# Causal linear attention in 64-token chunks instead of 128-token tiles, on one core of a Trainium2

## The reference

```python
q, k, v = (phi(qkv[0]), phi(qkv[1]), qkv[2])      # phi(x) = elu(x) + 1
def step(carry, inp):
    S, z = carry
    q_t, k_t, v_t = inp
    S = S + k_t[..., :, None] * v_t[..., None, :]
    z = z + k_t
    num = einsum('bhde,bhd->bhe', S, q_t)
    den = maximum(sum(z * q_t, axis=-1, keepdims=True), EPS)
    return (S, z), num / den
out = einsum('bld,ed->ble', out, w_out)
x = x + ga * out                                   # then the experts on layernorm(x)
```

## Time and profile before

| | |
|---|---|
| median of 3 runs | 864.46 us (862.91 to 868.9) |
| profiled execution, span | 864.3 us |
| PE busy | 812.9 us, 94% of the span |
| DVE, ACT, POOL busy | 577.1, 488.9, 478.9 us |
| instructions | 24637 |

### The profile page before, as it was taken

One profiled execution on the slowest core, in us unless ns is written; L12 is line 12 of the kernel. 1 busy time (PEld: TensorE's weight loads), 2 busy tenths in 40 slices (PEclk: granted clock), 3 DMA queues, 4 the chain that ended last, 5 costly groups with the idle time before them and its releaser, 6 DMA issues.

```text
span 864.3 us, 24637 instructions
## 1 busy us (share of the span) xinstructions
PE 812.9 (94%) x9527; PEld 667.7 (77%) x9527; DVE 577.1 (67%) x1740; ACT 488.9 (57%) x1003; POOL 478.9 (55%) x621
## 2 busy tenths in 40 slices
PE   6899999999999999999999999868999998999994
PEld 4677776777767767777777677558999998999994
DVE  5676676777777867868767767750756655767762
ACT  4665666656757656657657565442655453555551
POOL 2203345664664665646656646564556657666654
PEclk9999999999999999999999999988999999999997
DMA  5589903333332233322222212334476666676653
GB/s 195 186 247 282 284 26 114 85 87 110 67 120 89 76 114 87 86 101 70 72 71 62 64 50 41 62 85 148 82 158 120 151 145 122 152 152 158 121 100 37
DMA packets 71426, 99.02 MB, mean 115 GB/s; under 512 B 7810, under 2 KB 52866, under 8 KB 71320
## 3 DMA queue, kind: packets, MB, share of 16 engines
q1 hardware_dynamic: 38744, 53.93, 23.0%
q0 software_dynamic: 21760, 31.66, 16.2%
q10 hardware_dynamic: 10816, 11.96, 4.5%
HBM read 46.84 MB, written 63.36 MB: 127 GB/s over the span
## 4 chain that ended last, share of the span: by engine, by line
PE 75%; POOL 6%; DMA 6%; DVE 4%; issue 4%; ACT 3%; POOLq 0%; another core or an unknown queue 0%; SPq 0%; DVEq 0%; ACTq 0%
PE PJ L1436 10%; PE SCW L1662 9%; PE MD L1409 7%; PE SCW L1340 7%; PE SCW L1376 7%; PE PJ L1446 5%; PE SCW L1677 4%; PE SCW L1360 4%; PE SCW L1401 4%; DMA out<-EX,desti 3%; PE MD L1350 3%; PE SCW L1366 2%; PE SB L1677 2%; PE MD L1677 2%; POOL hT L544 2%
## 5 line engine op out<-in xcount | busy, mean ns | idle before, releaser
L494 POOL DMA_INDIRECT slot_rows<-Hrow,sloti x128 | 128.0, 1000 | 129.6 <-PE SCW L1366 48.5
L967 DVE TENSOR_TENSOR Sm<-SCW,tri 128x1024 f32<-128x1024 f32 x128 | 150.7, 1219 | 70.9 <-PE SCW L1340 69.0
L612 POOL DMA_INDIRECT out<-EX,desti x80 | 125.3, 1566 | 24.1 <-POOL idle L440 11.4
L1436 PE MATMUL PJ<-hT,w_qkv 128*128 128x512 f32 x384 | 110.1, 419 | 2.4 <-POOL hT L544 1.9
L440 POOL TENSOR_TENSOR idle<-mhalf 128x1 f32<-128x1 f32 x136 | 58.9, 433 | 78.5 <-DVE EX L1270 47.2
L1436 PEld LDWEIGHTS PJ<-hT,w_qkv 128*128 128x128 f32 x384 | 69.7, 190 | 25.1 <-issue 6.5
L1376 PE MATMUL SCW<-Sm,VA 128*17 128x128 f32 x2048 | 80.8, 275 | 0.2 <-issue 0.2
L1409 PE MATMUL MD<-w_og,ATs 128*128 128x256 f32 x256 | 73.2, 404 | 4.7 <-ACT ATs L824 2.8
L676 ACT ACTIVATE EX<-PJ 128x512 f32<-128x512 f32 x64 | 37.9, 592 | 67.5 <-PE PJ L1436 67.5
L1340 PE MATMUL SCW<-QM,KT 32*128 32x256 f32 x1024 | 73.3, 400 | 0.6 <-ACT OTs L839 0.5
L680 ACT ACTIVATE N<-X,nb,rs 128x256 f32<-128x256 f32 x128 | 66.4, 591 | 12.3 <-POOL nb L554 12.2
(11 more groups left out here) (215 smaller groups left out, 1825.4 us busy)
## 6 DMA issues: line engine op xcount, KB each, us to landing
Hrow<-slot_rows SPq DMA_DIRECT2D x32, 516.0 KB
slot_rows<-erow ACTq DMA_DIRECT2D x1, 10400.0 KB, 46.7
X<-x SPq DMA_DIRECT2D x16, 512.0 KB, 4.8
out<-X SPq DMA_DIRECT2D x16, 512.0 KB
Hrow<-mod_rows SPq DMA_DIRECT2D x16, 512.0 KB
QT<-slot_rows SPq DMA_DIRECT2D x8, 516.0 KB
slot_rows<-Hrow,sloti POOLq DMA_INDIRECT x128
N<-wd SPq DMA_DIRECT2D x4, 512.0 KB
```

Of the source, the lines that this page charges most:

```text
L494: pool.indirect_dma_start(xe, bass.IndirectOffsetOnAxis(sloti[:, par, k, t:t + 1], 0), Hrow[:, par, t, :], None, bounds_check=last_slot, o ...
L612: pool.indirect_dma_start(out, bass.IndirectOffsetOnAxis(desti[s % 2][:, a:a + 1], 0), Ys[s % 2][:, a, :], None, bounds_check=TOK - 1, oob ...
L967: dve.tensor_tensor(o.rearrange("p c (k w) -> p c k w", k=2), SCW[:, 2 * pair:2 * pair + 2, :].rearrange("p k (c w) -> p c k w", c=DC), tr ...
L1436: last = mm(PJ[m % 2][:], w_qkv[:, wp, cc, m * P:(m + 1) * P], hT[:, hp, cc, :], start=(cc + i == 0), stop=(cc == DC - 1 and i == len(SPLI ...
```

## The change

The chunk in which the attention is exact within itself shrinks from 128 to 64 tokens; a slot still holds one tile, which is two chunks (k = 0, 1).

- `scores` makes, for each chunk, 64 keys by 64 queries for two parities of heads: 16 matmuls of 32 rows x 64 columns of the array that stream 128 columns, instead of 8 of 32 x 128 that stream 256. The masked scores are 1024 numbers per partition instead of 2048, and DVE masks them with one instruction.
- `from_state` has 16 matmuls that stream 64 columns instead of 8 that stream 128: each chunk has its own state.
- `from_tile` has 32 matmuls of 64 rows x 17 columns (placed as 64 x 32) that stream 64 columns, instead of 16 of 128 rows that stream 128, and is no longer split.
- `add_to_state` has 16 matmuls of 64 rows instead of 8 of 128, into PSUM banks that it overwrites, and runs one tile ahead (tile n+1 in slot n). DVE masks both chunks' sums (`Snew`), then adds them one after the other to the state in SBUF (`Sbd`, now four states), three instructions instead of one. The product with the identity is gone.
- The keys of tile n+1 and the columns of tile n-1 are transposed together (`columns_and_keys`, four transposes), and ACT copies both with one instruction of 512 numbers instead of two of 256.
- `head_rows` moves to the end of the attention part of the same tile's slot, and DVE normalises the heads in that slot.
- PSUM: MD and PJ1 are now the two halves of PM, and each also takes the sums of one chunk; the output product goes to SB. So `add_to_state` waits until PJ1 has been read, and the late part of stage 1, the transposes of stage 1, the logits and `head_rows` wait for the new semaphore `state_read`. Several of POOL's sends of rows wait for other semaphores than before, and the second layer norm's scales are made one slot earlier.

```diff
+CH = P // 2
-        tri = sb("tri", [P, 2, P])
+        tri = sb("tri", [P, P])
+        tri64 = sb("tri64", [P, CH])
-        PJ = [ps("PJ0"), ps("PJ1")]
+        PJ0 = ps("PJ0")
+        PM = ctx.enter_context(nc.psum_tensor("PM", [P, 2, 512], F32))
+        PJ, MD = [PJ0[:], PM[:, 0, :]], PM[:, 1, :]
...
+            def columns_and_keys(n):
+                c0, c1 = (0 if tile_ok(n - 1) else D), (2 * D if tile_ok(n + 1) else D)
+                act.wait_ge(ak_full, n + 2)
+                at_least(act, op_full, n - 1)
+                at_least(act, state_full, n + 1 if tile_ok(n) else n)
+                act.activation(AK[:, c0:c1], MD[:, c0:c1], ACT.Copy).then_inc(ak_done, 1)
...
+            def masked_scores(T):
+                dve.wait_ge(sc_full, T + 1)
+                at_least(dve, av_done, T - 1)
+                dve.tensor_tensor(Smh(T % 2), SCW[:, :, 0:2 * P].rearrange("p r (m i) -> p r m i", i=CH),
+                                  tri64[:].unsqueeze(1).unsqueeze(1).to_broadcast([P, 4, 4, CH]),
+                                  ALU.mult).then_inc(sm_done, 1)
...
+            def state(n, first, second):
+                t = n + 1
+                dve.wait_ge(state_full, t + 1)
...
+                dve.tensor_tensor(Snew[:], PM[:, :, 0:DC * 2 * SW].rearrange("p k (h w) -> p k h w", h=DC * 2),
+                                  headmask[:].unsqueeze(1).to_broadcast([P, 2, DC * 2, SW]), ALU.mult
+                                  ).then_inc(state_read, 1)
...
+                dve.tensor_tensor(state_at(2 * t + 1), state_at(2 * t), Snew[:, 0], ALU.add).then_inc(sbd_half, 1)
...
+                    dve.tensor_tensor(state_at(2 * t + 2), state_at(2 * t + 1), Snew[:, 1], ALU.add).then_inc(sbd_done, 1)
...
+            def scores(T):
+                pe.wait_ge(q_masked, 2 * T + 2)
+                at_least(pe, ot_done, T)
...
                 for cc in range(DC):
+                    for k in range(2):
+                        for r in range(4):
...
+                            last = mm(SCW[part(k), r, cc * P:(cc + 1) * P],
+                                      KT[rows, gp, cc, q * P + CH * k:q * P + CH * k + CH],
+                                      QM[rows, T % 2, :, cc, part(k)], start=True, stop=True, skip_group_check=True)
...
+            def columns_and_keys(n):
...
+                    pe.wait_ge(an_done, n)
...
+                        last = pe.transpose(MD[:, cc * P:(cc + 1) * P], a[:, cc * P:(cc + 1) * P], ident[:])
...
+                    at_least(pe, ak_done, n + 1)
...
+                        last = pe.transpose(MD[:, D + cc * P:D + (cc + 1) * P],
+                                            KT[:, (t // 4) % 2, cc, (t % 4) * P:(t % 4 + 1) * P], ident[:])
...
+            def from_tile(T):
...
+                for cc in range(DC):
+                    for b in range(2):
+                        for k in range(2):
+                            for a in range(4):
+                                r, s = 2 * b + a // 2, a % 2
+                                last = mm(OB[32 * a:32 * a + SW, k, b, cc, :], VA[part(k), gp, q, head(cc, r, s), :],
+                                          Smh(T % 2)[part(k), r, 2 * cc + s, :], start=False, stop=True,
+                                          skip_group_check=True)
...
+            def add_to_state(n, g, routed, step):
...
+                pe.wait_ge(ak_done, n + 2)
...
+                        if n % 4 == 1:
+                            pe.wait_ge(h_raw, 2 * N + 2)
+                        else:
+                            pe.wait_ge(pj_read, 6 * N + 2 * (n % 4) - 2)
...
+                    if routed and step == "columns":
+                        pe.wait_ge(h2t_done, 2 * g + 2)
+                    if routed and step in ("first", "pick"):
+                        pe.wait_ge(taken, g + 1)
...
+                for cc in range(DC):
+                    for k in range(2):
+                        for r in range(4):
...
+                            last = mm(PM[32 * r:32 * r + 32, k, cc * 2 * SW:(cc + 1) * 2 * SW],
+                                      Kn[part(k), cc * P + 32 * r:cc * P + 32 * r + 32],
+                                      VA[part(k), gp, q, h:h + 2, :].rearrange("p s w -> p (s w)"),
+                                      start=True, stop=True, skip_group_check=True)
...
             def head_rows(T):
-                pe.wait_ge(ot_done, T)
-                at_least(pe, x1_done, T - 1)
+                pe.wait_ge(ot_done, T + 1)
+                pe.wait_ge(state_read, min(T + 2, TILES))
```

485 lines of the change are left out of this document (227 added, 258 removed).

## The result

The changed kernel takes 928.14 us, the median of 4 runs (924.81 to 929.81), against 865.19 us for the kernel before (4 runs, 862.91 to 868.9) on the same chip: a ratio of 1.073, 95% interval 1.069 to 1.077. The forecast was 831 us, the range 797 to 862, and 0.09 stood on slower. Nearly all of the 63 us lies in the attention stage: from the first to the last start of the scores pass 592.0 us (30.0 to 622.0), and 531.0 before (25.7 to 556.7). (Some executions of a kernel take over 1.5% longer than its fastest; medians here count them, ratios leave them out.)

What follows compares the result with a forecast made beforehand. The prediction took PE's list of steps to bound the kernel: -4.9 + 0.8 + 1.35 + 0.7 = -2.05 us per group, over 16 groups -33 us, from 864.3 to 831 us; range 797 to 862.

Steps and rivals of the forecast that it cites:

- What bounds the kernel: Attention stage: PE's own list of steps sets the time, busy 33.61 of 34.86 us of one group.
- PE's steps: PE's attention steps fall from 3.66 to 2.48 us a tile, identity product gone: 4.9 us saved per group.
- the form: PE step time is streaming rounds on side-by-side array places plus a rest; from the tile and sums 0.78 us.
- Instruction supply: From the tile and sums: small matmuls outrun the pace at which instructions arrive, +0.8 us per group.
- Instruction fetches: PE's 16 KB instruction packets: 1.7 times as many, partly visible in the small-matmul block, +1.35 us per group.
- Handovers: Waits between engines in the new order, chiefly add_to_state and stage 1's transposes: +0.7 us per group, bounds 0 to 2.
- A: Rival: PE's instructions keep up, no supply loss, fetches hidden as today; -4.25 us per group, 796 us, chance 0.20.
- B: Rival: only four array places work side by side, scores and from the tile stream as before; 851 us, chance 0.10.
- C: Rival: ACT becomes late for the slot, a quarter of a microsecond in every slot; 847 us, chance 0.12.
- D: Rival: small-matmul block runs at the arriving pace and every fetch shows; +1.7 us per group, 892 us, chance 0.13.
- L1389 plus L1422: Sign: product from the tile plus the sums on PE take near 1.0 us between starts.
- "issue" waits of PE: Sign: PE's waits for nothing the profile shows become about four times as many, in block L1374 to L1422.

Runs made afterwards that it cites:

- e13: Changed kernel with tile sums before the product from the tile in every slot, only the first two gate fills, output writes after the last tile: 886.0 us, ratio 1.033.
- e5: Changed kernel with the tile sums moved ahead of the product from the tile in every slot, not only q = 0: 906.7 us, ratio 1.049.
- e3: Changed kernel with only the first two gate fills and all output writes held back until the attention stage's last tile: 903.0 us, ratio 1.048.
- e7: Kernel before with its four attention products cut into as many matmuls as the changed kernel, without SyncE's bulk transfers in the attention stage: 923.3 us, ratio 1.069.
- e16: e15 with only the first two gate fills and output writes after the last tile: 902.2 us, ratio 1.057.
- e15: Changed kernel, sums first, half the fills, tile-wise writes, ScalarE reordered; output product behind sums, head rows between halves of late stage 1: 916.7 us, ratio 1.074.
- e9: Changed kernel with 32 more transposes on PE before the first tile, shifting the later code: 937.5 us, ratio 1.088.
- e6: Kernel before, order, tile and transfers kept, with its four attention products cut into as many matmuls as the changed kernel: 938.2 us, ratio 1.085.

## Why the prediction was wrong

**What bounds the kernel**: right. PE's list set the time before, and what hit PE hit the whole.

**PE's steps**: right in each step that can be read. Scores 0.63 (0.60 predicted), from the state 0.63 (0.60). From the tile and the sums together: in the slot with q = 1 at 310 us, from the tile starts at 311.01 and the output product at 312.06, so 1.05 us against the 0.78 that the form gave.

**Instruction supply**: right in kind, a little low: in that slot 1.05 less 0.78 is 0.27 us a tile, 1.1 a group, where 0.8 was taken. Steps and supply together were -4.1, and 33.61 - 29.49 is -4.1 too, but that is chance: the group of the earlier trace rows is one of the busiest of before. Against the same group before, the undisturbed one is busy for 3.5 us less, and against the mean of the stage (514.88 / 15.75 = 32.7) for 3.2.

**Instruction fetches**: this is the step that failed. "Their visible part is between 0.4 us (the share of today) and 3.2 (0.5 each)", taken as 1.35 a group. The count was right, 113 packets for the whole program against 72. The price of one was not. Waits for nothing in the stage, without those of the logits, are 56.9 us against 3.5, 3.4 us a group more, and the matmuls at the lower clock behind them cost another 1.2, so 4.6, beyond the upper bound. I took the 0.5 us that one stall showed behind matmuls of the old size for the most that a fetch can cost. A wait for an uncovered fetch is 1.1 to 2.0 us (1.62 in e13's row), because PE's stock of small matmuls lasts some 1 us of the 2.2 to 2.9 from the packet's start to PE's next record; and 2.7 to 5.7 us in six places where a 512 KB transfer of SyncE is ahead of it, which nothing in the term allowed for. The lower clock (0.50 in the third window) had no term either: it was put at nothing without a reason.

**Handovers**: too low. The rest of PE's idle time in the stage is 51.0 us (40.0, and 11.0 at the logits), against 11.9 before: +2.5 a group in place of +0.7, over the upper bound of 2. The sentence that failed is that the head rows are "covered by the sums and the output product (over 1.3 us)". That copy of the results was covered; but the head rows write the bank that the sums' copy (L1005) must first read, and its semaphore came 1.3 us late in 22 of 64 tiles: 17.2 us in all, 1.1 a group, and 21 us back in e5. The logits' wait for ScalarE's second read (11.0 us) was not in the list at all.

**The rivals.** A (instructions keep up) and B (only four places) are excluded by the rows above. C: ScalarE was late at the logits only. D had the mechanism, supply and fetches over 4.2 us a group, and came nearest with 892; it too had priced a fetch by the old stall. With what the stage shows, the sum is -3.2 (steps and supply) + 3.4 (fetches) + 1.2 (clock) + 2.5 (handovers) = +3.9 us a group, 61 us, the stage's whole loss.

**What would have shown it**: scores at 0.60, L1389 plus L1422 near 1.0 and one mask of 1.22 us were met (0.63, 1.05, 1.219). The "issue" waits of PE were to be four times as many; from 3.1 us in the waits before (100 to 500 us) they rose to 40.4 without the logits, thirteen times as much.

What stays open: why the sums' semaphore is late behind the product from the tile in two slots of four, what ScalarE's 10.4 MB cost (no run moved it), what the writes held back in e3, e7, e13 and e16 cost in the kernel before (it was not run so; its own waits for nothing, 3.5 us, leave little to gain), and 10 us of the loss in e15 behind the stage. Stage lengths are those of one profiled execution each.

## What to carry to other kernels

Count instructions as a resource of their own: before cutting long matmuls into small ones, ask how long the work at hand lasts while the next 16 KB of instructions come, some 2.5 us here, and price each fetch that falls into the dense block at the difference, not at the stall that long matmuls show today. Look then at which bulk transfers can be under way at that moment, since they turned stalls of 1.6 us into ones of up to 5.7 here. Count also what the lower clock takes from the work behind a long stall. Read the length of the stage beside the time: without SyncE's transfers 35 of 61 us came back in the stage, and only 22 in the time. And where a product hands over through a semaphore on which the next step's bank depends, try an order in which other matmuls follow it: that one move was worth as much here as a third of the loss.

## What the runs showed of the hardware

- A packet of instructions came only when a 512 KB transfer of SyncE's queue was nearly through (6.5 us with no instruction packet), and PE resumed 2.3 us after its start; without such a transfer ahead 2.6 us.
- All 19 waits for nothing of over 1 us ended 2.2 to 2.8 us after an instruction packet's start and stood at multiples of 125 matmul records; with 32 records put ahead the stall stood 31 records earlier in the work (e9).
- After a stall of 4.6 us, 4 us of matmuls ran at a granted clock of 0.50; over the stage the mean was 0.95 in place of 1.00, and matmuls took some 19 us longer.
- The semaphore of the sums took effect 1.8 us after the first of their records in one order and 0.54 in another, also when PE did nothing behind them.
- Cutting the four attention products into twice as many matmuls made a group longer by 3.1 us (33.34 to 36.42) where no long stall fell (e6).
- In 12 groups without bulk transfers of SyncE and without the late semaphore, the chunks of 64 tokens took 398.8 us where the tiles of 128 took 408.0 (e13).
